# A two-layer transformer step on one core: the first sequence's setup in smaller pieces, written-out engine orders, and probability products one key block at a time

## The reference, cut to what matters

```python
xn = layernorm(x)
x = x + attn0(xn) + ffn0(xn)      # attn0: biases, rmsnorm of q and k per head, sigmoid gate, output product
xn = layernorm(x)                 # ffn0: a shared expert, and 16 experts of width 64, the best 2 of a token
x = x + attn1(xn) + ffn1(xn)      # attn1: plain; ffn1: 8 experts of width 352, the best 2 of a token
# attention of one head: softmax(q @ k.T / sqrt(8), axis=-1) @ v
```

## Time and profile before

| | us |
|---|---|
| median of 3 runs | 666.58 |
| lowest and highest | 660.72, 666.75 |
| the profiled execution | 668.67 |
| its span, first to last instruction | 666.9 |
| PE busy in it | 600.8 (90%) |
| DVE, ACT, POOL busy | 491.6, 442.6, 307.6 |

### The profile page before, as it was taken

One profiled execution on the slowest core, in us unless ns is written; L12 is line 12 of the kernel. 1 busy time (PEld: TensorE's weight loads), 2 busy tenths in 40 slices (PEclk: granted clock), 3 DMA queues, 4 the chain that ended last, 5 costly groups with the idle time before them and its releaser, 6 DMA issues.

```text
span 666.9 us, 12167 instructions
## 1 busy us (share of the span) xinstructions
PE 600.8 (90%) x3764; PEld 322.5 (48%) x3764; DVE 491.6 (74%) x1088; ACT 442.6 (66%) x843; POOL 307.6 (46%) x422
## 2 busy tenths in 40 slices
PE   2554899899999999999999899999999999999994
PEld 1332233363655455445347557545656557666421
DVE  3789969688887788989876776976558786566632
ACT  3343265776688878877777767657766676676683
POOL 3153863278122557356748432357535622221443
PEclk9775758899999999999999999989999999999998
DMA  8442214353434443633652833536574645463111
GB/s 245 135 149 79 87 43 140 115 162 121 133 104 140 136 131 112 179 116 113 223 182 74 258 98 103 186 108 210 156 216 142 201 131 159 132 186 87 30 37 44
DMA packets 74895, 90.03 MB, mean 135 GB/s; under 512 B 6864, under 2 KB 62288, under 8 KB 74832
## 3 DMA queue, kind: packets, MB, share of 16 engines
q1 hardware_dynamic: 70736, 80.87, 40.3%
q0 software_dynamic: 4096, 8.40, 4.3%
HBM read 66.04 MB, written 22.81 MB: 133 GB/s over the span
## 4 chain that ended last, share of the span: by engine, by line
PE 72%; DVE 14%; ACT 6%; issue 3%; DMA 2%; POOL 1%; SPq 0%; DVEq 0%; POOLq 0%; ACTq 0%
PE pv_ps L977 17%; PE slot L947 15%; PE slot L964 14%; PE slot L924 8%; PE slot L937 6%; DVE mx L1345 5%; ACT probsT L1107 3%; PE slot L985 2%; PE slot L912 2%; PE slot L847 2%; PE slot L904 1%; PE slot L876 1%; PE slot L956 1%; ACT xn L1018 1%; DMA yg<-ys_hbm,index 1%
## 5 line engine op out<-in xcount | busy, mean ns | idle before, releaser
L1345 DVE TENSOR_REDUCE mx<-slot 128x1 f32<-128x512 f32 x512 | 324.0, 681 | 98.0 <-PE slot L947 97.4
L1107 ACT ACTIVATE probsT<-slot 128x512 f32<-128x512 f32 x512 | 274.8, 600 | 56.0 <-PE slot L964 55.4
L947 PE MATMUL slot<-k_stack,q_stack 72*128 72x512 bf16 x512 | 200.8, 397 | 10.0 <-DVE mx L1345 8.9
L964 PE MATMUL slot<-q_stack,k_stack 75*128 75x512 bf16 x512 | 192.8, 390 | 9.9 <-ACT probsT L1107 5.1
L977 PE MATMUL pv_ps<-probsT,v 128*32 128x512 f32 x1024 | 127.9, 617 | 0.2 <-ACT probsT L1107 0.2
L1439 POOL TENSOR_TENSOR hid<-th,up 128x512 f32<-128x512 f32 (+2 forms) x56 | 71.0, 1272 | 100.9 <-DVE th L1208 60.7
L947 PEld LDWEIGHTS slot<-k_stack,q_stack 72*128 72x128 bf16 x512 | 50.4, 99 | 97.8 <-DVE mx L1345 42.7
L964 PEld LDWEIGHTS slot<-q_stack,k_stack 75*128 75x128 bf16 x512 | 50.0, 99 | 77.6 <-ACT probsT L1107 30.8
L1427 POOL DMA_INDIRECT yg<-ys_hbm,index x64 | 62.1, 971 | 47.3 <-issue 22.9
L1416 POOL DMA_INDIRECT xs_hbm<-xn,index x64 | 63.5, 993 | 35.6 <-DVE index L1322 20.0
L924 PE MATMUL slot<-xgT,wbuf 128*128 128x128 f32 (+1 forms) x552 | 73.5, 275 | 2.4 <-DVE mx L1345 2.4
(11 more groups left out here) (131 smaller groups left out, 580.5 us busy)
## 6 DMA issues: line engine op xcount, KB each, us to landing
wbuf<-in_experts SPq DMA_DIRECT2D x46, 544.0 KB, 4.6
q_stack<-parts_hbm SPq DMA_DIRECT2D x32, 288.0 KB
k_stack<-parts_hbm SPq DMA_DIRECT2D x96, 96.0 KB
wbuf<-in_experts SPq DMA_DIRECT2D x62, 128.0 KB, 2.3
parts_hbm<-parts SPq DMA_DIRECT2D x16, 384.0 KB, 3.5
xg<-xs_hbm SPq DMA_DIRECT2D x24, 256.0 KB, 3.6
ys_hbm<-ys SPq DMA_DIRECT2D x24, 256.0 KB, 3.2
xs_hbm<-zeros SPq DMA_DIRECT2D x2, 2048.0 KB, 12.8
```

The source lines that it names most:

```text
L947: nc.tensor.matmul(ps[:, 0:N], q_stack[0:STACK, h, j * P:(j + 1) * P], k_stack[0:STACK, h, :], start=True, stop=True).then_inc(slot_full, 1)
L964: nc.tensor.matmul(ps[:, 0:N], k_stack[0:STACK + MAXROWS, h, j * P:(j + 1) * P], q_stack[:, h, :], start=True, stop=True).then_inc(slot_fu ...
L1107: nc.scalar.activation(probsT[:, k % PROBS, a, :], ps[:, 0:N], ACT.Exp, scale=SCALE).then_inc(slot_free, 1)
L1345: nc.vector.tensor_reduce(mx[:, g, u // J, u % J:u % J + 1], ps[:, 0:N], AXIS.X, ALU.max)\
```

## The change

- **probsT** has 3 buffers in place of 4, and a PV stage takes one key block: 128 stages of 8 instructions in place of 64 of 16. The exp of block k waits for PV of block k - 3.
- **Orders** of all engines are strings, and so is the slot of each PE stage; the planner goes. The set of stages is the same but for the changes below.
- **Pass 0's setup**: SQ and the sum of squares become SJ, once per token tile behind its bias addition. PT on DVE becomes RE (remainder, DVE), MI (the middle part, ACT copy of the remainder) and PT (the last part, DVE).
- **ZERO** reads rows of 2048 values out of `probsT[:, 0]`, zeroed at the start on DVE; `zeros` shrinks to one column; a fifth constant is waited for, and the first exp waits for both ZERO DMAs. The second ZERO stands further back in SP's order.
- **x** of pass 1 is loaded by a DMA of its own, x of passes 2 and 3 behind `w_shared`.
- **Orders, beginning and end**: PE has the four QV of pass 0 directly behind XT, ahead of SG and SU; ahead of its first E stand 9 QV, 3 XT and 27 M. ACT has SS of pass 0 ahead of GS, SG and SU. DVE has PT, QV, RT, LN, RW, SS, SL, NM behind each other and then the first M. The 128 PV stages stand in 120 groups. At the end DVE has the last YC ahead of the last AT, and XA last.

```diff
-PROBS = 4
-PER = 2
+PROBS = 3
+PER = 1
+CONSTS = 5
...
+ORDER = {
+    "PE": """
+XT QV4 XT SG SU SG QK2 QV4 SU RK M3 QK M4 SD M5 SD M5 XT M QK M NT M5 QV M3 E3 QV M E2 M E4 M3 E M5 PV M PV E NT
...
+E PV E2 M2 E M E2 M E PV E4 M PV E7 NT PV E2 PV AT E2 PV E8 PV E3 PV2 E3 AT E4 AT E2 PV E PV3 AT
+""",
+    "ACT": """
+XN XT XN XT SS GS SG SU SG QK HI QK HI MI2 SU RT SS QK XN HI QK NT XT E2 HI E8 NT E3 XN E11 SS PO E4 XT E2 QK NT
...
+    "DVE": """
+LN2 QV SJ QV SJ QV SJ QV SJ HAND NM GA2 QV RE2 GS PT2 QV3 RT LN RW SS SL NM M3 LN M14 SD SW M4 SD M QV M5 QV M12
...
+GA M GA M5 AT2 YC M7 GA M GA2 M2 HAND M15 AT GA M GA M GA M12 AT XA M16 YC AT3 YC AT XA
+""",
+    "POOL": """
+LN2 SQ GA LN GA SC BO SC BO PT MP LN BO SC4 MP PT SQ SC MP SC MP PT BO PT MP SQ GA SC2 GA SC GA SC MP SC2 GA3 MP
...
+    "SP": """
+ZERO PW RF WL RF WL RF WL ZERO NT WL2 RF NT WL2 PW WL3 RF WL NT WL5 XL2 RF WL XL WL NT2 XL RF WL7 PW XL YS XL WL
...
-        zeros = sb("zeros", [P, D])
+        zeros = sb("zeros", [P, 1])
...
-            sp.dma_start(x[:, J:T], x_tiles[:, J:T]).then_inc(x_rest_in, 16)
+            sp.dma_start(x[:, J:2 * J], x_tiles[:, J:2 * J]).then_inc(x1_in, 16)
             sp.dma_start(w_shared[:], hbm["w_shared"]).then_inc(loaded, 16)
+            sp.dma_start(x[:, 2 * J:T], x_tiles[:, 2 * J:T]).then_inc(x_rest_in, 16)
...
-                    sp.dma_start(hbm[f"xs{r}"].rearrange("(b p) d -> p b d", p=P),
-                                 zeros[:].unsqueeze(1).broadcast_to([P, NB[r // 2], D])).then_inc(zeroed[r], 16)
+                    sp.dma_start(hbm[f"xs{r}"].rearrange("(p c n) d -> p c (n d)", p=P, c=2),
+                                 probsT[:, 0].rearrange("p h t -> p (h t)").unsqueeze(1).broadcast_to([P, 2, HG * N]))\
+                      .then_inc(zeroed[r], 16)
...
+                elif kind == "MI":
+                    a = stage[1]
+                    sc.wait_ge(rest_done, a + 1)
+                    nc.scalar.activation(parts[:, a, 1], rest[:, a], ACT.Copy).then_inc(mid_done, 1)
...
+                    if a == 0 and k == 0:
+                        sc.wait_ge(zeroed[0], 16)
+                        sc.wait_ge(zeroed[1], 16)
...
+            nc.vector.memset(probsT[:, 0], 0.0).then_inc(consts_set, 1)
...
+                elif kind == "SJ":
+                    j = stage[1]
+                    ve.wait_ge(*emptied(("QV", 0, j)))
+                    of_tile = slice(2 * j * D, 2 * (j + 1) * D)
+                    sq = squares[:].rearrange("p a t -> p (a t)")[:, of_tile]
+                    link(nc.vector.tensor_tensor(sq, qk_tok[:, of_tile], qk_tok[:, of_tile], ALU.mult))
+                    last = nc.vector.tensor_reduce(mean_sq[:, 2 * j:2 * j + 2], sq.rearrange("p (x d h) -> p x h d", d=HD, h=H),
+                                                   AXIS.X, ALU.add)
+                    if j == J - 1:
+                        last.then_inc(ms_done, 1)
+                elif kind == "RE":
+                    a = stage[1]
+                    ve.wait_ge(hi_done, a + 1)
+                    nc.vector.tensor_tensor(rest[:, a], qk[:, a], parts[:, a, 0], ALU.subtract).then_inc(rest_done, 1)
                 elif kind == "PT":
                     A, a = stage[1:]
-                    ve.wait_ge(hi_done, 2 * A + a + 1)
-                    nc.vector.tensor_tensor(rest[:, a], qk[:, a], parts[:, a, 0], ALU.subtract)
-                    link(nc.vector.tensor_tensor(parts[:, a, 1], qk[:, a], parts[:, a, 0], ALU.subtract))
+                    ve.wait_ge(rest_done, a + 1)
+                    ve.wait_ge(mid_done, a + 1)
                     nc.vector.tensor_tensor(parts[:, a, 2], rest[:, a], parts[:, a, 1], ALU.subtract)\
                         .then_inc(parts_done, 1)
```

More of the change, by code:

```diff
@@ L51, in seq @@
     return A % B
[L54 to L157, removed]
@@ L182, in buffer_of @@
     return ((r % 2) * NB[r // 2] + b) % WBUF[r // 2]
[L185 to L195, removed]
-        if (engine, kind) in MOVES or (engine, kind, layer_of(stage)) in MOVES:
-            self.moves, self.lands = MOVES.get((engine, kind)) or MOVES[engine, kind, layer_of(stage)]
-        if kind in ("XG", "GU", "GG", "UU", "DN") and engine == "PE":
-            short = len(blocks_of(stage[1] // 2, stage[2])) / 4
-            self.holds, self.lasts = self.holds * short, self.lasts - self.holds * (1 - short)
-        self.start = self.end = None
@@ new lines, in order_of @@
+def order_of(engine, gated):
+    order, left = [], {"GA": [("GA", *stage) for stage in gated]}
+    for word in ORDER[engine].split():
+        kind = word.rstrip("0123456789")
+        if kind not in left:
+            left[kind] = stages_of(kind)
+            if (engine, kind) in PART_OF:
+                left[kind] = left[kind][PART_OF[engine, kind]]
+        queue = left[kind]
+        for _ in range(int(word[len(kind):] or 1)):
+            order.append(queue.pop(0))
+    assert not any(left[kind] for kind in left if kind != "GA" or engine in ("DVE", "POOL")), left
+    return order
@@ L550 @@
 class Plan:
     def __init__(self):
-        self.orders, self.ring, gated, _ = engine_orders()
-        self.gated_stages = gated
-        self.gated = {stage: n for n, stage in enumerate(gated)}
+        self.orders = {"PE": order_of("PE", [])}
+        self.gated_stages = [stage for stage in self.orders["PE"] if stage[0] in ("SG", "GU", "GG")]
+        self.gated = {stage: n for n, stage in enumerate(self.gated_stages)}
+        for engine in ("ACT", "DVE", "POOL", "SP"):
+            self.orders[engine] = order_of(engine, self.gated_stages)
@@ L558, in __init__ @@
+        fills = [stage for stage in self.orders["PE"] if stage[0] in FILLS]
+        self.ring = {fill: int(k) for fill, k in zip(fills, "".join(SLOT.split()), strict=True)}
         self.nth = {}
         uses = [0] * SLOTS
-        for stage in self.orders["PE"]:
-            for fill in fills_of(stage):
-                self.nth[fill] = uses[self.ring[fill]]
-                uses[self.ring[fill]] += 1
+        for fill in fills:
+            self.nth[fill] = uses[self.ring[fill]]
+            uses[self.ring[fill]] += 1
```

418 lines of the change are left out of this document (123 added, 295 removed), and 23 rows, old and new, of tables (HOLDS, LEAN, SHIFT).

## The result

The changed kernel runs in 644.06 us (median of 4 runs, 640.09 to 645.58), the kernel before beside it in 664.59 (4 runs, 660.72 to 666.75). The ratio is 0.9688, with a 95% interval of 0.9619 to 0.9757: 3.1% faster. The forecast was 660, with a range of 648 to 673.

The account below looks back on a forecast made before the run. PE was taken to set the pace, busy 438.7 of 450 us between 150 and 600 us. 668.67 - 11.7 + 12.9 - 5.4 - 2.4 = 662.1 us profiled, 660.0 as a median; range 648 to 673.

Parts of the forecast that it names:

- first E earlier: Start of the E stream on PE: first E at 68.0 us, 15.1 us earlier than before.
- work owed: PE work not yet done at the earlier first E (QV, XT, M): 3.4 us, leaving -11.7 net.
- Steps 1 to 4: Start: constants +0.7, QV first and squares by tile -3.1, parts by two engines -2.3, router: first E 15.1 us earlier.
- step 3: Pass 0's parts split over DVE and ACT: -2.3 us; POOL's SQ, sharing SBUF interfaces, might take up to 1 us back.
- Rival 4: Start: first E comes no earlier, as ACT or POOL is late for NM or MP: 671.7 us; chance 0.08.
- Rival 2: DVE queue holds PE up between the 48th and 96th M; gain 5 instead of 11.7: 666.7 us; chance 0.20.
- The PV term: PV stages on PE: 56 more entries into 128x32 stages at 0.23 us each, +12.9 us.
- ZERO, the loads and the buffers: ZERO from 8 KB rows and split x loads: 0; three buffers stopping ACT: a rival at 674 us, chance 0.12.
- the end term: End of the kernel: last YC ahead of the last AT, store following XA, -2.4 us.
- Finer PV, and orders in the open time (-5.4): PE from 150 to 600 us: shorter PV stages and new orders take half of 11.3 us open time, -5.4.
- Rival 1: Orders remove all open time on PE and 5 us of entries cost nothing: 649 us; chance 0.20.

Follow-up runs that it names:

- a_same: The changed kernel, unaltered, run again as a reference: 644.19 us, 0.9649 of the kernel before.
- a_pieces_2: The changed kernel with whole square, whole sum and all three parts on DVE in pass 0: 645.14 us, 0.968 of the kernel before.
- a_orders: The changed kernel with two-block PV stages, 4 buffers and pass 0's setup in whole pieces: 655.95 us, 0.9852 of the kernel before.
- b_spread: The kernel before with each PV stage cut in halves, the first half four E stages earlier, 4 buffers: 682.2 us, ratio 1.0276.
- a_zeros: The changed kernel with both ZERO DMAs early, from 512-byte rows, without the memset of probsT: 643.43 us, 0.9672 of the kernel before.
- a_four_2: The changed kernel with 4 probsT buffers in place of 3: 644.93 us, 0.9683 of the kernel before.
- a_end: The changed kernel with YC of the last sequence behind XA again: 647.38 us, 0.9687 of the kernel before.
- a_pairs: The changed kernel with two-block PV stages and 4 buffers, each at the place of the second half: 654.63 us, 0.985 of the kernel before.
- a_pairs_lead3_2: The changed kernel with two-block PV stages and 4 buffers, each at most three E behind its last block: 676.24 us, 1.019 of the kernel before.
- b_replan_2: The kernel before with single-block PV stages and three buffers, its own planner laying out the order: 679.88 us, ratio 1.0221.
- a_hid_later: The changed kernel with the memset of hid moved behind the first LN: 644.68 us, 0.9647 of the kernel before.
- a_again: The changed kernel, unaltered, run as a reference for other comparisons: 645.54 us, 0.9692 of the kernel before.

## Why the prediction was wrong

The terms of the forecast beside what the profile of `a_same` shows, whose span is 23.2 us under that of the kernel before, near the difference of the medians:

| term | forecast | measured |
|---|---|---|
| first E earlier | -15.1 | -16.8 |
| work owed | +3.4 | +3.5 |
| PV entries | +12.9 | +12.0 |
| open time | -5.4 | -18.8 |
| end | -2.4 | -3.0 |
| sum | -6.6 | -23.1 |

**Steps 1 to 4 held.** Every station of the start came within 1.2 us until the mask, and the first E 1.7 to 2.8 us earlier than forecast; `a_pieces_2` and `a_orders` show that the smaller pieces are worth about 3 us of it. The rule weighed in step 3 took nothing back: POOL's SQ begins at 33.71, behind the parts, and the last two subtractions took 1.29 us together. Rival 4 didn't happen. Rival 2's waits are there, 5 to 7 us at the full clock between the 48th and the 96th M, but the kernel before has 8.5 between the same two, so they take nothing from the gain.

**The PV term held.** 1.31 us around a stage of eight, 57 more entries, 0.21 each. `b_spread` shows it by itself: 64 more entries, 13.4 us more in entries, 17 us slower. Here the rule weighed in the forecast (the Trainium skill, TensorEngine Tiling (Array Packing), Key Properties: a changed tiling mode drains TensorE) agrees with the row, which has 0.09 us in and 0.10 out.

**ZERO, the loads and the buffers held** (`a_zeros`, `a_four_2`), and so did the end term (`a_end`; 3.0 for 2.4).

**The step that failed is "Finer PV, and orders in the open time (-5.4)".** It measured -18.8, and that is 13.4 of the 16.5 us missed. The clock isn't the reason: at the full clock the fall is 18.1 us. By the forecast's own measure the step came out well, since idle time from 150 to 600 us went from 11.3 to 5.2 us, and "half of it gone" is about right by starts too (18.1 of 41.7 us). But half was a choice that no row bore out, so that much is luck; what failed is what it was half of. Two things were wrong in it. The bound was: "-11.3 (all open time gone)" took the idle time of the earlier trace rows for all the open time there is, and by starts there are some 30 us in the same window, 37.6 behind 140 us and 56.1 in all. The Trainium skill (Perfetto Trace Analysis, opening note on judging a kernel's closeness to the roofline) calls matmul busy time a bad metric, because matmuls are pipelined; the rows at 159 us bear it out, with 0.38 us bars 0.22 us apart, and the forecast used that metric all the same. And the step took the length of a stage and its order for two things with an effect each. The runs say otherwise:

| other waits at the full clock (all), us | order not laid out for it | laid out by the old planner | written out |
|---|---|---|---|
| pairs | | before 42 (56) | `a_pairs` 45 (56), `a_orders` 42 (58), `a_pairs_lead3_2` 58 (79) |
| single blocks | `b_spread` 42 (59) | `b_replan_2` 32 (40) | changed kernel 24 to 25 (33 to 41) |

Of the 18.1 us at the full clock, 9.8 come as soon as single blocks have an order laid out for them, with the planner of the kernel before. The other 8.3 come with the written order. Behind 140 us, where the start has no part, it is the same: 36 us before, 26 with the planner, 16 to 17 with the written order. So each does about half, and the orders' half shows only with single blocks. The written orders are also worth the start, and an end that the planner spoils for single blocks (23.3 us behind PE's last matmul, against 4.5). That single blocks are needed isn't shown: an order written and searched for pairs, which might take waits away too, wasn't tried.

Why a single block in its place takes waits away is only argued. The reading that fits is an even supply. In these PE rows of `a_same` no stage of other work takes over 1.1 us, and M and E come in small groups between them:

```profile
163.70 0.38 PE L633 MATMUL slot<-k_stack,q_stack 72*128 72x512 bf16 x1
163.92 0.59 PE L650 MATMUL slot<-q_stack,k_stack 75*128 75x512 bf16 x2
164.35 0.38 PE L633 MATMUL slot<-k_stack,q_stack 72*128 72x512 bf16 x1
164.57 0.38 PE L650 MATMUL slot<-q_stack,k_stack 75*128 75x512 bf16 x1
164.79 1.05 PE L569 MATMUL slot<-w_shared,hid 128*128 128x128 f32 x8
165.68 0.38 PE L633 MATMUL slot<-k_stack,q_stack 72*128 72x512 bf16 x1
165.90 0.81 PE L650 MATMUL slot<-q_stack,k_stack 75*128 75x512 bf16 x3
166.64 1.07 PE L663 MATMUL pv_ps<-probsT,v 128*32 128x512 f32 x8
167.64 0.60 PE L633 MATMUL slot<-k_stack,q_stack 72*128 72x512 bf16 x2
```

The M start 0.65, 1.33 and 1.96 us apart, and DVE, at 0.61 for one, holds none of them; in the kernel before M and E alternate behind a stage of 16, which would be an M every 0.44 us, and go at DVE's 0.60. One stretch of each isn't proof, and a count over all M behind 140 us doesn't bear it out: distances of 0.57 to 0.66 us from M to M are 39 in the kernel before and 40 in `a_same`. What the table by stages says is where the waits went, most of them ahead of an E (14 to 5 us) and an M (10 to 3); why stays open. Rival 1 (649, "the orders do more than half") came nearest, but it too was bounded by the 11.3 us, and its 5 us of entries that cost nothing didn't come.

No variant was clearly faster than the changed kernel: `a_zeros` and `a_hid_later` lie within its interval.

## What to carry to other kernels

When an engine is pipelined, measure what it waits by the distance from start to start against its unhindered spacing, and not by idle time: a share of 97% busy hid most of 30 us here. Split that sum by the granted clock before comparing two kernels: here single profiles of one kernel differed by 8 us in all, and by 1 us at the full clock. A smaller stage has a price that can be read from the trace beforehand (its entries), but its worth shows only with an order laid out for it, so testing one half of such a change alone can find a loss (`b_spread`) or no gain in waits (`a_pairs`). And of a variant that loses, look where: `b_replan_2` was 2% slower in total and 5.4 us ahead on PE.

## What was not expected of the hardware

A cost of entering and leaving isn't seen at PV stages alone: the NT stage (128 rows, 12 columns out) stands at 0.09 us in and 0.095 out too, by the same starts.

On one chip (the kernel before at 688.34 us in place of 665 to 666) DVE, ACT and PE each stop for up to 4 to 5.9 us with "issue" or "remote" as the reason (the profile shows no releaser), and kernels that are 3% faster elsewhere are not faster there.

The share of full clock differs between profiles of the same kernel: the time at a granted 0.5 within the span was 37.5 us in the first profile of the changed kernel (span 638.2), 54.8 in `a_same` (643.7) and 64.4 in `a_again` (647.4). The spans go with it, and so does nearly all of the difference between 33 and 41 us of other waits; in the kernel before it was 77.0 us.
